# Four images at a time for the plain energies, a value bias moved to the residual rows, and engine orders written across layers

## The reference

```
layer 0 (plain attention):  q = x Wq + bq, k = x Wk + bk   (16 channels each)
                            a = softmax(q k^T)             (256 x 256 per image)
                            x = gamma * (a (x Wv + bv)) + x
layer 1 (mixer):            xh = DHT2d(x); two block-diagonal products with relu,
                            soft shrinkage by 0.01, DHT2d back, + x
layer 2 (plain attention):  as layer 0, with its own weights
layer 3 (normed attention): group norm (32 groups), q, k, v of 128 channels,
                            softmax(q k^T / sqrt(128)) v Wo + bo, + x
```

## Time and profile before

| | |
|---|---|
| median of 3 runs | 123.65 us (121.46 to 125.22) |
| the profiled execution's own time | 121.65 us |
| its span, first to last instruction | 119.8 us |
| granted TensorE clock over the span | 1.00 of full speed |
| busy: PE, PEld | 102.2 us (85%), 83.6 us (70%) |
| busy: DVE, ACT, POOL | 65.5 us (55%), 61.8 us (52%), 44.9 us (37%) |
| chain of work that ended last | PE 64%, DVE 10%, ACT 8%, POOL 6%, DMA 5%, issue 4% |

### The profile page before, as it was taken

The page is one execution under the profiler, slowest core; times in us unless marked ns, Lnnn a source line. Parts: engine busy times, 40 slices in busy tenths (PEclk is TensorE's granted clock), DMA queues, the critical chain, the costliest instruction groups (busy, mean ns, idle before and its releaser), DMA issues.

```text
span 119.8 us, 2207 instructions
## 1 busy us (share of the span) xinstructions
PE 102.2 (85%) x748; PEld 83.6 (70%) x748; DVE 65.5 (55%) x220; ACT 61.8 (52%) x166; POOL 44.9 (37%) x89
## 2 busy tenths in 40 slices
PE   6859899899996897779799999797898599999770
PEld 5446678889994796557588677676777499999450
DVE  0048748676494356544486287383558276666511
ACT  4006615454557485564169473757545366666510
POOL 0106600000055043224305234368764979553400
PEclk9999999999999999999999999999999999999999
DMA  3999000000000000000000000000000001111211
GB/s 60 277 334 401 24 0 5 0 0 3 5 0 0 0 3 0 5 0 0 0 0 5 0 0 0 0 3 5 0 0 3 0 16 43 40 39 41 75 56 44
DMA packets 3034, 4.46 MB, mean 37 GB/s; under 512 B 464, under 2 KB 2128, under 8 KB 3024
## 3 DMA queue, kind: packets, MB, share of 16 engines
q1 hardware_dynamic: 2016, 3.34, 8.3%
q10 hardware_dynamic: 1008, 0.99, 2.7%
HBM read 3.28 MB, written 1.05 MB: 36 GB/s over the span
## 4 chain that ended last, share of the span: by engine, by line
PE 64%; DVE 10%; ACT 8%; POOL 6%; DMA 5%; issue 4%; ACTq 0%; DVEq 0%
PE banks L600 9%; PE banks L547 8%; PE banks L515 7%; PE banks L572 6%; PE banks L594 5%; DMA values<-in_values 5%; PE banks L555 4%; PE banks L646 4%; PE banks L672 4%; PE banks L499 3%; DVE lowest L1065 3%; PE banks L616 3%; POOL probs L409 3%; PE banks L659 3%; ACT probs L882 3%
## 5 line engine op out<-in xcount | busy, mean ns | idle before, releaser
L409 POOL TENSOR_TENSOR probs<-probs,inverse 128x256 f32<-128x256 f32 x32 | 19.0, 614 | 20.6 <-DVE inverse L1081 20.6
L399 POOL TENSOR_SCALAR acts<-first,head 64x260 f32<-64x260 f32 x8 | 10.1, 1269 | 34.9 <-DVE first L1136 34.9
L888 ACT ACTIVATE probs_t<-banks 128x512 f32<-128x512 f32 x24 | 14.3, 597 | 15.4 <-PE banks L572 15.4
L882 ACT ACTIVATE probs<-banks,lowest 128x256 f32<-128x256 f32 x32 | 14.0, 472 | 14.1 <-DVE lowest L1065 14.1
L600 PE MATMUL banks<-probs_t,v 128*128 128x256 f32 x64 | 17.1, 390 | 1.6 <-ACT probs_t L888 1.6
L572 PE MATMUL banks<-ident,probs 128*128 128x128 f32 x96 | 15.0, 275 | 1.9 <-POOL probs L409 1.7
L600 PEld LDWEIGHTS banks<-probs_t,v 128*128 128x128 f32 x64 | 11.4, 190 | 4.5 <-ACT probs_t L888 2.9
L572 PEld LDWEIGHTS banks<-ident,probs 128*128 128x128 f32 x96 | 11.3, 142 | 3.4 <-issue 1.8
L1065 DVE TENSOR_REDUCE lowest<-banks 128x2 f32<-128x512 f32 x16 | 10.3, 685 | 5.8 <-PE banks L515 5.8
L1073 DVE TENSOR_SCALAR_CACHE_REDUCE negated<-banks,v 128x256 f32<-128x256 f32 x16 | 7.1, 482 | 7.4 <-PE banks L555 7.3
L515 PE MATMUL banks<-qk 32*128 32x256 f32 x64 | 9.1, 400 | 0.0
(11 more groups left out here) (108 smaller groups left out, 199.2 us busy)
## 6 DMA issues: line engine op xcount, KB each, us to landing
out<-stream SPq DMA_DIRECT2D x7, 128.0 KB, 1.9
rows<-in_x_rows SPq DMA_DIRECT2D x1, 768.0 KB, 9.9
xt_in<-in_x_t SPq DMA_DIRECT2D x2, 256.0 KB, 4.7
xt_in<-in_x_t SPq DMA_DIRECT2D x1, 512.0 KB, 6.6
constants<-in_constants SPq DMA_DIRECT2D x1, 462.0 KB, 8.2
layer<-in_layer ACTq DMA_DIRECT2D x1, 256.5 KB, 10.0
values<-in_values ACTq DMA_DIRECT2D x2, 128.0 KB, 7.6
rows<-in_x_rows ACTq DMA_DIRECT2D x1, 256.0 KB, 7.7
```

The source lines that it names most:

```text
L399: pool.tensor_scalar(acts[H2:C, image % 4, 1], partners(flat(first[H2:C, image % 2]), SUMS, -SUMS, SUMS), column["b1n"][H2:C], 0.0, ALU.ad ...
L409: pool.tensor_tensor(probs[:, at, tile, :], probs[:, at, tile, :], inverse[:, at, tile:tile + 1].to_broadcast([TILE, TOKENS]), ALU.mult).t ...
L882: nc.scalar.activation(probs[:, at, tile, :], of, ACT.Exp, bias=lowest[:, at, tile:tile + 1], scale=sign, **sums).then_inc(probs_ready, 1)
L888: nc.scalar.activation(flat(probs_t[:, job.image % 4]), probs_t_bank, ACT.Copy).then_inc(probs_t_ready, 1)
```

## The change

1. `strip_energies` takes four images: all four row strips, first for tile 0, then for tile 1. Images 4 to 7 wait until all exponents of images 0 to 3 are read out of the banks. Layer 2 moves one energy bank from 2 to 6.
2. Layer 0's value bias: `values0` holds the weight only, a new load `bias0` the bias rows. POOL multiplies both by gamma (`gate_values0`, `gate_bias0`) and adds the bias to the residual rows of each image (`add_bias0`). The values are then evicted without a bias, by ACT instead of DVE. Values and sums of layer 0 use banks 5 and 7 in turn for the first images.
3. A buffer per image in place of rotating ones (`u`, `v`, `v3`, `negated`, `lowest`, `probs`, `total`, `inverse`, `probs_t`, `z`, `of_sums`, `first`, `acts`, `g`); the mixer's `y_top` and `y` use `xt_in` and `normed`. Waits that guarded the rotation go. Semaphores are counted per layer. The transposed probabilities of layers 2 and 3 use bank 2 instead of 6; layer 3's energies rotate over three banks instead of two.
4. Loads on ACT's queue: `head` (layer 0's strips and gamma only), `values0` (64 KB), `ident`, rows of images 0 and 1, `bias0`, `layer2` (strips, value weight and columns), `layer3` (with the output bias).
5. The loops that ordered the four engines are replaced by flat lists in which steps of neighbouring layers alternate.

The core of the diff:

```diff
             def strip_energies(layer, image):
-                pair = [Job(layer, image), Job(layer, image + 1)]
-                pe.wait_ge(strips_ready, strips_of(pair[0]))
+                quad = [Job(layer, image + k) for k in range(QUAD)]
+                pe.wait_ge(strips_ready, strips_of(quad[-1]))
...
+                elif image:
+                    pe.wait_ge(probs_ready[layer], QUAD * TILES)
                 for tile in range(TILES):
-                    for job in pair:
+                    for job in quad:
...
+            def gate_values0():
+                pool.wait_ge(head_loaded, 16)
+                pool.wait_ge(values0_loaded, 16)
+                pool.tensor_tensor(vw0[:, :], values0[:, :], gamma0.to_broadcast([C, C]),
+                                   ALU.mult).then_inc(values0_gated, 1)
+            def add_bias0(i):
+                pool.wait_ge(bias0_gated, 1)
+                pool.wait_ge(x_loaded[0 if i < X_LOADS[0][1] else 1], 16)
+                pool.tensor_tensor(rows[:, i], rows[:, i],
+                                   vb0[:, :].unsqueeze(1).to_broadcast([TILE, TILES, C]),
+                                   ALU.add).then_inc(bias0_added, 1)
...
 # POOL's order: gate_values0, halves, diagonals(0), diagonals(1), identity_plus,
 # gate_bias0, add_bias0(0..5), attention_rows, add_bias0(6), add_bias0(7),
 # activate_upper(0..7), scale_probs(2,0..4), place_stats(0), scale_probs(2,5),
 # norm_scales(0), place_stats(1), normalize(0), scale_probs(2,6), normalize(1),
 # norm_scales(1), normalize(2), place_stats(2), normalize(3), scale_probs(2,7),
 # scale_probs(3,0), norm_scales(2), normalize(4), normalize(5), scale_probs(3,1), ...
...
 # PE, from the first strips
+            project_strips(0, (0, 1))
+            project_v(Job(0, 0))
+            project_strips(0, (2, 3))
+            project_v(Job(0, 1))
+            project_v(Job(0, 2))
+            strip_energies(0, 0)
+            project_v(Job(0, 3))
+            project_v(Job(0, 4))
+            project_v(Job(0, 5))
+            project_strips(0, range(QUAD, BATCH))
+            project_v(Job(0, 6))
+            project_v(Job(0, 7))
+            transpose_probs(Job(0, 0))
+            prepare("mixer0")
+            strip_energies(0, 4)
...
+            transpose_probs(Job(0, 3))
+            mix_values(Job(0, 2))
+            forward_tokens(0)
+            transpose_probs(Job(0, 4))
+            prepare("stacked")
+            first_product(0)
+            forward_tokens(1)
+            prepare("y_bias")
+            mix_values(Job(0, 3))
...
 # PE, middle of the mixer
+            second_product(3)
+            backward_tokens(0)
+            backward_channels(2)
+            first_product(6)
+            backward_tokens(1)
+            project_v(Job(2, 0))
+            backward_channels(3)
...
 # PE, end
+            energies(Job(3, 7))
+            transpose_probs(Job(3, 5))
+            mix_values(Job(3, 4))
+            transpose_probs(Job(3, 6))
+            mix_values(Job(3, 5))
+            transpose_probs(Job(3, 7))
+            mix_values(Job(3, 6))
             mix_values(Job(3, 7))
...
 # ACT, layer 0
-                if i % 2 == 0:
-                    if i >= 2:
-                        move_probs(Job(0, i - 2))
-                    exponents(Job(0, i))
...
+            move_v(Job(0, 3))
+            exponents(Job(0, 0))
+            move_v(Job(0, 4))
+            exponents(Job(0, 1))
+            move_v(Job(0, 5))
+            exponents(Job(0, 2))
+            exponents(Job(0, 3))
+            move_probs(Job(0, 0))
...
 # DVE, start and middle of the mixer
-            nc.vector.tensor_scalar(values0[:, :], values0[:, :], column["gamma0"], None,
-                                    ALU.mult).then_inc(values0_gated, 1)
             take_strips(0, (0, 1))
-            dve.wait_ge(values0_gated, 1)
-            move_v(Job(0, 0))
+            take_strips(0, (2, 3))
             highest(Job(0, 0))
             highest(Job(0, 1))
...
+            add_turned(0)
+            shrink(3)
+            add_turned(1)
+            partners_results(6)
+            activate(6)
+            add_turned(2)
+            shrink(4)
```

More of the change, by code:

```diff
@@ L95, with tiles_before @@
 JOBS = [Job(layer, image) for layer in range(LAYERS) for image in range(BATCH)]
[L98 to L106, removed]
+def tiles_before(job):
+    return job.image * TILES
 STRIPS = [Job(0, 0), Job(0, 2), Job(0, 4), Job(2, 0), Job(2, 4)]
@@ L466, in _ @@
[L466 to L478 removed]
+            gate_values0()
@@ L492, in project_strips @@
                     pe.wait_ge(layer_done[MIXER], BATCH)
-                at = 0 if layer == 0 else HEAD
+                weights = head if layer == 0 else layer2
                 for which in range(2):
@@ L1186, in _ @@
-            for i in range(BATCH):
-                if i < 2:
-                    add_residual(Job(0, 6 + i))
-                if i >= 2:
-                    shrink(i - 2)
-                if i >= 4:
-                    add_turned(i - 4)
-                partners_results(i)
-                prepared_at(BATCH + i)
-                if i == 7:
-                    take_strips(2, range(QUAD))
-                activate(i)
+            highest(Job(0, 2))
+            highest(Job(0, 3))
+            take_strips(0, range(QUAD, BATCH))
@@ new lines, in _ @@
+            take_prepared("mixer0")
+            highest(Job(0, 4))
+            add_residual(Job(0, 0))
+            highest(Job(0, 5))
+            add_residual(Job(0, 1))
+            take_prepared("mixer1")
+            highest(Job(0, 6))
+            highest(Job(0, 7))
+            add_residual(Job(0, 2))
+            take_prepared("stacked")
+            take_prepared("y_bias")
+            partners_results(0)
+            add_residual(Job(0, 3))
+            partners_results(1)
+            activate(0)
@@ new lines, in _ @@
+            add_residual(Job(0, 4))
+            activate(1)
+            take_prepared("weights3")
+            gate_values2()
+            partners_results(2)
+            add_residual(Job(0, 5))
+            take_prepared("values3")
+            shrink(0)
+            partners_results(3)
+            activate(2)
+            activate(3)
+            add_residual(Job(0, 6))
+            partners_results(4)
+            shrink(1)
+            add_residual(Job(0, 7))
+            take_prepared("bias3")
@@ L1199, in _ @@
+            shrink(2)
+            activate(4)
+            partners_results(5)
+            activate(5)
+            add_turned(0)
[5 more added lines that the diff above has]
+            shrink(4)
+            add_turned(3)
+            shrink(5)
+            partners_results(7)
+            take_strips(2, range(QUAD))
             shrink(6)
+            activate(7)
             add_turned(4)
             highest(Job(2, 0))
-            highest(Job(2, 1))
+            shrink(7)
```

937 lines of the change are left out of this document (554 added, 383 removed).

## The result

The changed kernel takes 102.22 us (median of 4 runs, 102.13 to 102.63); the kernel before, on the same chip, 123.39 us (121.46 to 125.22). The ratio is 0.837 with a 95% interval of 0.826 to 0.847. The forecast was 105.5 us with a range of 100.5 to 113.5. The profiled execution took 102.17 us, with a span of 100.3 us, against 121.65 and 119.8 before.

The account below looks back on a forecast made before the run. PE was taken as the bound, with 92.3 us of work and 19.8 lost. Start 4.7 + 92.3 - 4.2 (quads) + 8.0 lost + 2.85 after the last mix + 1.85 outside the span gave 105.5 us, range 100.5 to 113.5.

Parts of the forecast that it names:

- Quads: Energies: four groups of four images replace 8 pairs, each taking 1.06 us like one pair; gain 4.2 us.
- The bias: Layer 0's value bias: POOL's eight additions, 4.9 us, lie in its gap of 19.54 us; costed at nothing.
- Loads: Kernel start: value weight lands at 6.6 us, first values start at 7.2 instead of 7.44; gain 0.2.
- The mixer's stops: Mixer's middle: about 1.03 us in each of four turns, lost to DVE's written order, goes.
- What PE still loses: PE between first and last useful matmul: 8.0 us lost instead of 19.8, from 6.8 of stops and 1.2 of refilling.
- second quad: Layer 0: the second quad waits for all exponents of images 0 to 3; PE stops 0.8 us.
- merged stretch: Layer 0's tail merged with the mixer, DVE's list full for some 8 us: three stops, 1.0 us.
- layer 2 1.2: Layer 2: ACT's evictions, exponents and `v` per image take nearly PE's own 2 us; PE stops 1.2 us.
- layer 3's start: Group norm of images 0 and 1 runs during layer 2's PE work, POOL's list full; PE stops 0.3 us.
- Quads like pairs: Rival at the energies: quads run no better than pairs, price 4.2 us, time 109.7; chance 0.10.
- Stops that return: Rival: late evictions stop PE, which still loses 19.8 us; only quads and load pay, 117.3 us; chance 0.18.
- the convoy: Rival in merged stretch, layers 2 and 3: engines wait on each other, 1.03 us per image and stage, 130.2; chance 0.04.

Follow-up runs that it names:

- the halves together and apart: Changed kernel with each of the four energy groups split into two groups of two images, the following product between them: 106.71 us, against 102.2.
- the uncrossed borders: Changed kernel with all engines' lists sorted by layer at the border of layer 0 and mixer (112.31 us), of layers 2 and 3 (114.41), or all three (133.50).

## Why the prediction was right, and where its sizes were not

- **Quads.** Forecast 1.06 us each and a gain of 4.2; measured 1.08, and 4.5 us between the halves together and apart. Right, and for the reason given, although the row behind the 1.06 was one of strips packed by columns. That single-file loads would make it 2.9 us is refuted here; the section cited in the prediction prices one load, and there the trace agrees (184 ns for 32 rows, 190 for 128 in the mixes of layers 2 and 3); that loads add up was my own addition, not a rule against packing. The Trainium skill ("TensorE: Matmul & The Clock Gate", "Part 3: Packing small matmuls — row/col tiling") has the rule that applies: loads overlap with running matmuls when they go to other row groups. The traces agree: 16 matmuls in 1.08 us where 8 take 1.06.
- **The bias.** Costed at nothing, with POOL's gap as the cover. Doubling it cost nothing measurable, so the cover is shown; putting it back on DVE cost nothing either. The part was right as costed, but in this order it was not a source of the gain. ACT's listed busy time did not rise to 65 us as forecast; it is 61.3.
- **A buffer per image.** Costed at nothing; shown for the two buffers that were tried, open for the others and for the moved banks.
- **Loads.** This term was mis-sized. I put the weight's landing at 6.6 us, near the late end of its bounds, taking the other queue's loads as what sets it, and the first values at 7.2; it landed at 5.75 and they started at 6.43. The gain is 1.0 us between the two profiles and 1.4 to 1.5 with the load alone undone, not 0.2. The range had held it, the point in it was chosen badly.
- **The mixer's stops.** That the time was lost to the written order is shown by the exchange of two lines in the old kernel: 4.4 us, four turns at about 1.1.
- **What PE still loses.** The second mis-sized term: 8.0 forecast, 4.4 measured, which makes the whole of the 3.3 us between 105.5 and 102.2 (the other terms differ by 0.3 the other way); 0.7 of it is the earlier load. Both mis-sized terms err to the same side, so the total is not right by errors that cancel. The step that failed is the walk down the new lists: second quad 0.8, merged stretch 1.0, layer 2 1.2 and layer 3's start 0.3. The trace lists none of these four. I took a helper that is nearly full for one that stops PE. In the window from 60 to 70 us shown above, ACT is busy for 8.10 of 10 us, as full as I expected, and PE for 9.97. My reading is that enough products of other images stand between a step and its use; the uncrossed borders, where they do not, agree with it. The start (0.66 forecast as 1.4) and the end (from 92.01 to 97.30 for 3.5 us of work, 1.8 forecast as 2.1) came out nearer. What remains, 4.4 - 0.66 - 1.8 = 1.9 us, lies in gaps too short to be listed, for which I had 1.2.
- **Rivals.** Quads like pairs: refuted by 1.08 us. Stops that return and the convoy: no stop is listed between 7 and 96 us, and those above 0.3 us sum to 1.2 us where the prediction's sign was about 7. The borders' experiments turn the convoy around: with lists kept apart by layer the engines waited for each other.

Of the 19.5 us between the profiles, 4.5 go to the energies and 1.4 to the load, by undoing each in the changed kernel. The rest, 13.6, is the order with its buffers and banks, by subtraction; 4.4 of it is shown in the old kernel, and the remaining 9.2 were not isolated one by one. The timeline of the kernel before tells where most of them stood. Beside the mixer's turns, the first values and the end it lists nine stops, 6.4 us in all, or 7.8 with 0.16 us of end overlap for each, and the changed kernel lists none of them. Three of the nine, beside those of the earlier trace rows:

```profile
15.02 0.68 PE L547 MATMUL banks<-values,xt_in 128*128 128x128 f32 x4 [0.62 <-DVE v L1053]
...
38.76 0.63 PE L688 MATMUL banks<-ident,rows 128*128 128x128 f32 x4 [1.18 <-ACT stream L925]
...
84.89 0.67 PE L529 MATMUL banks<-normed,uw 128*128 128x256 f32 x2 [0.41 <-DVE moments L1116]
```

Which part of the order removed each was not tried. The border experiments show that crossing the layers is worth more than this in the changed kernel, but not that the crossing is the source.

## What to carry to other kernels

When one engine's work fills most of the span, price an order by a ledger of that engine's slots, and don't add a stop for every helper that is nearly full: ask instead what stands in the list between a step and its use. Packing row strips needs matmuls of different strips next to each other in the list, and cover for the wait that a larger group makes; without the cover it gained nothing here. Idle time can cost twice, once as itself and again as matmuls at the lower clock: after a stretch in which PE worked 1.00 of 5 us, the next 7 us ran at 0.58 of full speed, while the kernel before, whose longest listed stop between its layers is 1.66 us, kept a granted clock of 1.00.

## What the runs showed of the hardware that was not expected

- Two pairs of energies on different row strips, written one after the other, overlap fully: 16 matmuls in 1.09 us. With another product between them each pair takes 1.06 us.
- TensorE's level in the first microseconds differs between the profiled executions: the first strips, 8 matmuls, took anything from 1.06 to 1.92 us. In the kernel with two lines exchanged the lower level lasted until about 20 us while the profile states a granted clock of 1.00 for the span; only the durations of the matmuls show it.
